# An attention and mixture-of-experts layer on one core: the orders of the repeated step and of the last chunk rewritten on four engines

## What is computed

```python
x = L0_attn_x
xn = _layernorm(x, axis=-1)
# attention
x_tran = jnp.matmul(x, W) + b
weights = jnp.einsum('bsd,btd->bst', x_tran, x)
weights = jnp.exp(jnp.tanh(weights * lw)) * off_diag
weights = weights / (jnp.sum(weights, axis=-1, keepdims=True) + EPS)
return jnp.matmul(weights, x)
# experts: 8, of which the best 2 by sigmoid(x @ gate_w.T) + expert_bias; 176 hidden units each
h = jnp.square(jax.nn.relu(h.astype(jnp.bfloat16)))
routed_out = _masked_grouped_mm(h.astype(jnp.bfloat16), w_down.astype(jnp.bfloat16), onehot)
# shared expert, also 176 hidden units
hs = jnp.square(jax.nn.relu(xf @ shared_w_up.T))
shared_out = hs @ shared_w_down.T
# all of it
x = x + _L0_attn_ref(xn, ...) + _L0_ffn_ref(xn, ...)
```

## Time and profile before

| what | us |
|---|---|
| median of 3 runs (lowest, highest) | 120.36 (120.07, 120.89) |
| the profiled execution | 120.12 |
| its span, first to last instruction | 118.4 |

### The profile page before, as it was taken

How to read it: one execution, slowest core, us unless ns; L and a number is a source line. 1 busy time by engine, 2 the same in 40 slices (tenths; PEclk the granted TensorE clock), 3 DMA queues, 4 the chain that set the end, 5 groups by cost and what they waited for, 6 DMA issues and landing times.

```text
span 118.4 us, 2789 instructions
## 1 busy us (share of the span) xinstructions
PE 110.9 (94%) x912; PEld 84.1 (71%) x912; DVE 99.9 (84%) x316; ACT 89.0 (75%) x138; POOL 71.5 (60%) x121
## 2 busy tenths in 40 slices
PE   3977699999999999999999999999999999999981
PEld 3934346968768786878678776869587876778780
DVE  6996889888898989989888988988988688989821
ACT  4463699798579894989689876989499867996740
POOL 6459798999993389716991499436971603215000
PEclk9999999999999999999999999999999999999999
DMA  3999306628956939296848959393938757696962
GB/s 85 302 239 312 118 0 122 122 41 169 172 111 123 176 73 208 42 214 93 154 89 200 101 108 173 78 179 81 170 77 210 130 110 134 120 213 127 158 174 89
DMA packets 47821, 16.56 MB, mean 140 GB/s; under 512 B 44992, under 2 KB 45760, under 8 KB 47808
## 3 DMA queue, kind: packets, MB, share of 16 engines
q1 hardware_dynamic: 47232, 15.44, 64.8%
q0 software_dynamic: 288, 0.72, 3.5%
q10 hardware_dynamic: 288, 0.23, 0.9%
HBM read 3.84 MB, written 2.10 MB: 50 GB/s over the span
## 4 chain that ended last, share of the span: by engine, by line
PE 86%; DVE 8%; issue 2%; ACT 1%; POOL 1%; DVEq 0%; POOLq 0%; ACTq 0%
PE out_ps L925 16%; PE h_ps L878 14%; PE side L854 11%; PE dots L833 10%; PE out_ps L913 6%; DVE gated L639 5%; PE side L867 5%; PE out_ps L907 4%; PE small L823 4%; PE out_ps L955 4%; PE small L805 4%; PE small L790 2%; PE h_ps L891 2%; PE small L814 1%; PE side L823 1%
## 5 line engine op out<-in xcount | busy, mean ns | idle before, releaser
L639 DVE SCALAR_TENSOR_TENSOR gated<-h_ps,gates 128x1408 bf16<-128x1408 f32 x28 | 45.1, 1612 | 5.0 <-PE h_ps L878 4.5
L467 ACT ACTIVATE hidden<-gated 128x1408 bf16<-128x1408 bf16 x30 | 41.3, 1376 | 2.4 <-DVE gated L654 1.2
L925 PEld LDWEIGHTS out_ps<-downT,hiddenT 128*128 128x128 bf16 x341 | 21.5, 98 | 5.7 <-issue 3.4
L925 PE MATMUL out_ps<-downT,hiddenT 128*128 128x128 bf16 x341 | 23.9, 219 | 0.0
L257 POOL TENSOR_SCALAR xn<-x_sb,meanvar,rstd 128x128 f32<-128x128 f32 x28 | 22.1, 800 | 0.8
L878 PE MATMUL h_ps<-upT,xnTb 128*128 128x512 bf16 (+1 forms) x84 | 21.3, 362 | 0.7 <-DVE gated L639 0.5
L290 POOL TENSOR_SCALAR_AFFINE_SELECT probs<-probs 128x256 f32<-128x256 f32 x16 | 6.6, 411 | 20.0 <-ACT probs L424 20.0
L833 PE MATMUL dots<-projT,xnT 128*128 128x256 f32 x60 | 15.6, 382 | 0.6 <-ACT projT L415 0.6
L854 PEld LDWEIGHTS side<-xn,probs 128*128 128x128 f32 x120 | 15.0, 191 | 1.3 <-issue 0.5
L854 PE MATMUL side<-xn,probs 128*128 128x129 f32 x120 | 15.9, 275 | 0.0
L833 PEld LDWEIGHTS dots<-projT,xnT 128*128 128x128 f32 x60 | 10.7, 190 | 4.5 <-ACT projT L415 2.3
(11 more groups left out here) (105 smaller groups left out, 171.7 us busy)
## 6 DMA issues: line engine op xcount, KB each, us to landing
x_sb<-in_x SPq DMA_DIRECT2D x7, 256.0 KB, 8.8
out_y<-final SPq DMA_DIRECT2D x7, 256.0 KB, 4.1
hiddenT<-hidden SPq DMA_TRANSPOSE x31, 3.7
upT<-in_up POOLq DMA_DIRECT2D x1, 352.0 KB, 7.2
downT<-in_down POOLq DMA_DIRECT2D x1, 352.0 KB, 8.1
out_y<-final SPq DMA_DIRECT2D x2, 128.0 KB, 1.7
late_sb<-in_late SPq DMA_DIRECT2D x1, 192.0 KB, 5.6
x_sb<-in_x ACTq DMA_DIRECT2D x1, 128.0 KB, 2.8
```

Source lines behind the costliest of these rows:

```text
L467: a.activation(hidden[:, t, :], gated[:, t, :], ACT.Square).then_inc(squared, 1)
L639: v.scalar_tensor_tensor(out=gated[:, t, :].rearrange("p (e h) -> p e h", e=E), in0=h_ps[:, 0:NH].rearrange("p (e h) -> p e h", e=E), scal ...
L925: last = t_.matmul(out_at(t), hiddenT[:, c % 2, t, j, :], downT[:, j, :], start=(t == 0 and j == 0 and c < LAST), stop=((t >= 2 or c == LA ...
```

## The change

Nothing is computed differently. The routing scores of chunk 0 are kept in PSUM (`scores_at`), for which the first `route_scores` waits for `decay_copied` and the first `shared_main` for the first gates. POOL's early `normalize` calls are split by tile. Step k = 2 is written out with the calls and the order it had. For k from 3 on, and after the loop for the last chunk, the calls are the same and stand in another order on PE, DVE, ACT and POOL. SP's list stays.

```diff
--- before.py
+++ after.py
@@ -176,6 +176,11 @@
         def out_at(t):
             return out_bank(t // 2)[:, (t % 2) * P:(t % 2 + 1) * P]
 
+        def scores_at(c):
+            if c > 0:
+                return scores[:, :, :]
+            return out_ps[:, 0:TILES * E].rearrange("p (t e) -> p t e", t=TILES)
+
         def turn_at(part):
             return h_ps[:, part * CH:(part + 1) * CH].bitcast(BF16)
 
@@ -329,14 +334,19 @@
             normalize_fourth()
             narrow(0)
             rsqrt(1)
-            normalize(1)
+            normalize(1, 0, 1)
+            normalize(1, 1, 2)
+            normalize(1, 2, 3)
+            normalize(1, 3, 4)
             mask(0, 0)
             narrow(1)
             square_rest(0)
             rsqrt(2)
-            normalize(2, 0, 2)
+            normalize(2, 0, 1)
+            normalize(2, 1, 2)
             mask(0, 1)
-            normalize(2, 2, 4)
+            normalize(2, 2, 3)
+            normalize(2, 3, 4)
             make_gates(1)
             square_rest(1)
             square_shared(0)
@@ -347,21 +357,33 @@
             mask(1, 1)
             narrow_ident()
             narrow(2)
-            for k in range(2, NCH + 1):
...
+            for k in range(3, NCH + 1):
                 f, c = k, k - 1
                 if k + 1 < NCH:
                     rsqrt(k + 1)
+                if f < NCH:
+                    square_rest(f)
+                if k + 1 < NCH:
                     normalize(k + 1)
                 if f < NCH:
-                    square_rest(f)
-                add_x(c)
+                    make_gates(f)
                 square_shared(c)
                 if f < NCH:
-                    make_gates(f)
                     mask(f, 0)
-                    mask(f, 1)
+                add_x(c)
                 if k + 1 < NCH:
                     narrow(k + 1)
+                if f < NCH:
+                    mask(f, 1)
 
         @block.scalar
         def _(act):
@@ -410,6 +432,8 @@
                 a.activation(pair[:, :, 0:2], top8[:, :, 0:2], ACT.Copy).then_inc(pair_set, 1)
 
             def take_proj(c):
+                if c == 0:
+                    act.wait_ge(early_loaded, 16)
                 act.wait_ge(proj_made, c + 1)
                 wait(act, dots_made, Q * (c - 1))
                 a.activation(projT[:, c % 2, :], proj_bank(c)[:, :], ACT.Identity, bias=b_sb).then_inc(proj_taken, 1)
@@ -470,7 +494,6 @@
             take_xT(0)
             copy_decay()
             exp_logits(0)
-            act.wait_ge(early_loaded, 16)
             take_proj(0)
             take_pair(0)
             relu_rest(0)
@@ -496,16 +519,28 @@
             take_exp(1, 1)
             exp_logits(2)
             relu_rest(2)
-            for k in range(2, NCH):
...
+            for k in range(3, NCH):
                 f, c = k, k - 1
+                relu_rest(f)
+                exp_logits(f)
                 scale_attention(c)
-                if f >= 3:
-                    exp_logits(f)
-                    relu_rest(f)
                 square(c, 0)
                 square(c, 1)
+                take_proj(f)
                 take_pair(f)
-                take_proj(f)
                 relu_shared(c)
                 square(c, 2)
                 take_tanh(f, 0)
@@ -515,9 +550,9 @@
                 square(c, 3)
                 take_tanh(f, 1)
                 take_exp(f, 1)
+            scale_attention(LAST)
+            square(LAST, 0)
             relu_shared(LAST)
-            square(LAST, 0)
-            scale_attention(LAST)
             square(LAST, 1)
             square(LAST, 2)
             square_last()
@@ -588,7 +623,9 @@
             def route_scores(c):
                 dve.wait_ge(expT_taken, c + 1)
                 wait(dve, gates_ready, c)
-                v.reciprocal(scores[:, :, :], onep[:, :, :]).then_inc(topk_step, 1)
+                if c == 0:
+                    dve.wait_ge(decay_copied, 1)
+                v.reciprocal(scores_at(c), onep[:, :, :]).then_inc(topk_step, 1)
 
             def route_bias(c):
                 if c == 0:
@@ -597,7 +634,7 @@
                 bias = ebias.rearrange("p (a e) -> p a e", a=1).to_broadcast([P, TILES, E])
                 if c == 0:
                     dve.wait_ge(fillers_set, 2)
-                v.tensor_tensor(biased[:, :, 0:E], scores[:, :, :], bias, ALU.add).then_inc(topk_step, 1)
+                v.tensor_tensor(biased[:, :, 0:E], scores_at(c), bias, ALU.add).then_inc(topk_step, 1)
 
             def route_top(c):
                 then(c, 2)
@@ -615,7 +652,7 @@
 
             def route_gates_first():
                 dve.wait_ge(marks_set, 1)
-                v.scalar_tensor_tensor(out=gates[:, 0, :, :], in0=marked[:, :, 0:E], scalar=MARK, in1=scores[:, :, :],
+                v.scalar_tensor_tensor(out=gates[:, 0, :, :], in0=marked[:, :, 0:E], scalar=MARK, in1=scores_at(0),
                                        op0=ALU.is_equal, op1=ALU.mult).then_inc(gates_ready, 1)
 
             def weigh(c, q):
@@ -725,44 +762,63 @@
             attend_norm(0, 1)
             gate(0, 3)
             weigh(1, 1)
-            for k in range(2, NCH):
...
+            for k in range(3, NCH):
                 f, c, o, g = k, k - 1, k - 2, k + 1
                 gate(c, 0)
                 attend_sums(c, 0)
-                attend_norm(c, 0)
                 if g < NCH:
                     norm_stats(g)
+                attend_norm(c, 0)
                 gate(c, 1)
+                route_one(f)
                 finish(o, 0)
-                route_one(f)
+                route_scores(f)
                 attend_sums(c, 1)
-                route_scores(f)
+                route_bias(f)
                 attend_norm(c, 1)
-                route_bias(f)
                 attend(c)
                 route_top(f)
                 gate(c, 2)
+                weigh(f, 0)
                 route_mark(f)
-                weigh(f, 0)
                 gate(c, 3)
+                weigh(f, 1)
                 finish(o, 1)
-                weigh(f, 1)
             gate_halves(0)
             attend_sums(LAST, 0)
             attend_norm(LAST, 0)
             gate_halves(1)
+            gate_halves(2)
             finish(LAST - 1, 0)
-            gate_halves(2)
             attend_sums(LAST, 1)
+            finish(LAST - 1, 1)
             attend_norm(LAST, 1)
-            finish(LAST - 1, 1)
             gate_halves(3)
-            attend(LAST)
             at, to = PARTS[1]
             dve.wait_ge(turned, 2)
             dve.wait_ge(out_made, TILES * (LAST - 1))
             v.tensor_copy(hiddenT[:, LAST % 2, TILES - 1, at:to, :].rearrange("p j n -> p (j n)"),
                           turn_at(1)[:, 0:(to - at) * P]).then_inc(turned_taken[1], 1)
+            attend(LAST)
             finish(LAST, 0)
             finish(LAST, 1)
 
@@ -859,7 +915,7 @@
             def shared_main(c):
                 if c == 0:
                     pe.wait_ge(late_loaded, 16)
-                    pe.wait_ge(decay_copied, 1)
+                    pe.wait_ge(gates_ready, 1)
                 if c == LAST:
                     pe.wait_ge(proj_taken, c + 1)
                 elif c > 0:
@@ -977,47 +1033,65 @@
             dots(1, 1)
             transpose_x(2)
             down_tile(0, 0)
-            for k in range(2, NCH):
...
+            for k in range(3, NCH):
                 f, c, o = k, k - 1, k - 2
                 up_tile(c, 0)
                 attend(c, 0)
-                if k == 2:
-                    down_tile(0, 1)
+                shared_down_rest(o)
                 rest(f)
-                shared_down_rest(o)
                 up_tile(c, 1)
                 shared_down_main(o)
                 down_tile(o, 2)
                 transpose_exp(f)
                 attend(c, 1)
+                project(f)
                 up_tile(c, 2)
-                project(f)
-                down_tile(o, 3)
                 shared_main(c)
                 dots(f, 0)
+                down_tile(o, 3)
                 up_tile(c, 3)
-                down_tile(c, 0)
                 if f + 1 < NCH:
                     transpose_x(f + 1)
                 dots(f, 1)
+                down_tile(c, 0)
                 down_tile(c, 1)
             c, o = LAST, LAST - 1
             up_by_bank(0)
+            attend(c, 0)
             shared_main(c)
-            attend(c, 0)
             up_by_bank(1)
             shared_down_rest(o)
+            attend(c, 1)
+            up_by_bank(2)
             shared_down_main(o)
-            up_by_bank(2)
             down_tile(o, 2)
-            attend(c, 1)
             down_tile(o, 3)
             up_by_bank(3)
             shared_down_rest(c)
             shared_down_main(c)
             down_tile(c, 0)
+            turn_last()
             down_tile(c, 1)
-            turn_last()
             down_last()
             down_tile(c, 2)
 
```

(76 more changed lines are left out.)

## The result

| | before | after |
|---|---|---|
| median of 17 runs (lowest, highest), us | 120.46 (120.07, 120.98) | 119.69 (119.09, 120.09) |
| the profiled execution, us | 120.12 | 119.69 |
| its span, us | 118.4 | 117.9 |

The ratio of the changed kernel to the one before is 0.9927, with a 95% interval of 0.9909 to 0.9944. That is 0.73% less, or 0.88 us of 120.46 by the ratio; the two medians differ by 0.77. The forecast was 0.88 less and a median of 119.5, so the total is right to within 0.2. The way there is not: one term that was set to zero brought some 0.3 to 0.4, and one that was set to 0.46 was lost, wholly in the profiled execution and in part in others. The profile of the changed kernel shows both.

A forecast was written before the change was run, and what follows sets the result against it. PE was taken as the bound in the middle of the kernel. Steps 0.35 and last chunk 0.53, with the beginning at 0, made 0.88 off 120.36 us: 119.48, rounded 119.5, range 118.9 to 120.5.

The forecast's parts named there:

- PE bounds the steps and only neighbours count: Steps k = 3 to 7: PE's calls stay the same, so only their neighbours matter; 0.35 us less in sum.
- The swap of `rest` and `shared_down_rest` at 0, between -0.1 and +0.2: Steps 3 to 7: exchanging these two calls was priced at 0, with bounds of -0.1 to +0.2 us a step.
- The two close places: Repeated steps: `shared_main` waiting for bank `side`, 0.09 us left, and POOL's `mask` ahead of `attend(f, 0)`, 0.5 left.
- rival E: Steps: POOL's new wait for the marks makes PE's `attend(f, 0)` late; 121.7 us if 0.8 later than counted; chance 0.12.
- B: Gain eaten by a late last transposing DMA, or `shared_main` waiting for its bank in the steps; 120.0 to 120.4; chance 0.19.
- C: Steps: no load was exposed by its neighbour as read, so the order changes nothing there; 119.83 us; chance 0.06.
- The last chunk up to `turn_last`, 0.07: Last chunk: new neighbours for `attend(c, 1)` and `shared_down_main(o)` give net -0.06, rounded up to 0.07 us won.
- The beginning at 0: Beginning: scores in PSUM, split `normalize` and moved waits cost some hundredths either way; taken as 0.
- Rival D: Beginning: keeping the scores in PSUM ends the 0.52 us ahead of the first gate; 119.0 us; chance 0.13.
- The end at 0.46: End: `turn_last` before `down_tile(c, 1)` wins PE's idle 0.46 us, if ACT's square and the last DMA are in time.
- last chunk 0.53 forecast: Whole last chunk: 0.07 up to `turn_last` plus 0.46 at the end, 0.53 us less.
- the prediction's own signs of being wrong: PE idle ahead of `shared_main`, `attend` or the last down tile; swapped calls longer; the 0.52 ahead of the first gate gone.

The follow-up runs named there:

- e3_steps: The kernel before with the new order of steps 3 to 7 alone, beginning and last chunk as before; ratio to before 0.9975.
- e5_swap_back: The changed kernel with `rest(f)` again ahead of `shared_down_rest(o)` in steps 3 to 7; 119.52 us, ratio to before 0.9916.
- e1_scores: The kernel before with the scores of chunk 0 in PSUM and nothing else of the change; ratio to before 0.9961.
- e8_wait: The kernel before with only DVE's added wait for `decay_copied` in chunk 0's `route_scores`, scores left in SBUF; ratio to before 0.9971.
- e9_count63: The changed kernel with the memset of `pair` moved from DVE to POOL, one DVE instruction less ahead of the first gate; median 119.83 us, ratio to before 0.9935.
- e4_last: The kernel before with the new order of the last chunk alone; ratio to before 0.9971.

## Why the prediction came out right, and where it did not

- **PE bounds the steps and only neighbours count: right.** 0.35 forecast, 78.31 - 77.95 = 0.35 measured (78.307 - 77.952) in the changed kernel, and again in e3_steps. It divides as forecast too: 0.06 in each of the steps 3 to 6 and 0.11 in step 7. `shared_main` went from 0.91 to 0.86, `dots` of step 7 from 0.92 to 0.86.
- **The swap of `rest` and `shared_down_rest` at 0, between -0.1 and +0.2: right.** Same middle in e5_swap_back.
- **The two close places: in time.** The residual that frees the bank ended at 69.73 + 0.61 = 70.34, and `shared_main` started at 70.59, with no idle time ahead of it (DVE's timeline, after):

```profile
69.73 0.61 DVE L710 SCALAR_TENSOR_TENSOR resid<-side,rownorm,x_sb 128x128 f32<-128x128 f32 x2
```

  and POOL's timeline, after, shows the new wait for the marks, 1.85 long, and `mask` done at 75.86, where `attend(f, 0)` starts at 76.64, 0.78 later. I had counted 0.5 (my own numbers, 77.14 - 76.5, give 0.64):

```profile
73.86 0.31 POOL L273 TENSOR_SCALAR hot<-marked 128x32 f32<-128x32 f32 x1 [1.85 <-DVE marked L650]
...
75.45 0.41 POOL L295 TENSOR_SCALAR_AFFINE_SELECT probs<-probs 128x256 f32<-128x256 f32 x1
```

  So neither the bank nor the mask was late: rival E did not happen, nor the second half of B. The 0.35 of the steps excludes C.
- **The last chunk up to `turn_last`, 0.07: right, measured 0.06.** `shared_down_rest(c)` starts 8.16 after `up_by_bank(0)`, before 8.22. `attend(c, 1)` pays the 1.09 behind `shared_down_rest` and `shared_down_main(o)` is back at 0.89.
- **The beginning at 0: wrong, the term that was put too low.** Rival D had the place and the size (0.5; measured 0.41 ahead of the gate, 0.33 of it left at `up_tile(1, 0)`, 0.39% in e1_scores), but not the cause. It gave the place of the scores as the reason, and e8_wait and e9_count63 exclude it. The step that failed is "the price is some hundredths either way": the added wait was priced by what it waits for, and not as an instruction that shifts all behind it.
- **The end at 0.46: the move is right, the condition was missed.** The prediction made the gain depend on the landing of the last DMA and put it at the middle, 3.7. It did land in 3.61. But it was issued 0.8 late, because the issue ahead of it on SP took 2.85. I had taken the time of the issue from the square before it and had not asked what holds SP's queue. Rival B had the size: from the end of the square, 109.99, to the landing, 114.41, it is 4.42, and B's 0.6 for a landing of 4.4 is close to the 0.66 measured. Its sentence "the last transpose of the kernel before was in time" is true, but it was read off a kernel in which the packet came too late to hold that issue. How much is lost varies: 0.66 in the profiled execution (tail 16.35), less in those of e5_swap_back, e4_last and e9_count63 (15.99, 15.91, 15.87).
- **The sum.** In the terms of the forecast: steps 0.35 for 0.35; last chunk 0.53 forecast, -0.18 to 0.30 measured; beginning 0 forecast, 0.3 to 0.4 measured. The ratio gives 0.88 in all, the medians 0.77. Two errors of about the same size and opposite sign stand in the right total, and that is luck. Two of the prediction's own signs of being wrong are there: PE idle ahead of the last down tile behind the DMA, and the 0.52 ahead of the first gate gone.

The Trainium skill, "SBUF — State Buffer", section "Who interferes with whom", states that a DVE instruction with two SBUF inputs contends with a GpSimd instruction that reads SBUF. By that rule, keeping the scores in PSUM should free the first gates' making from POOL's `normalize`. No run here shows it. In the kernel before (DVE's timeline):

```profile
12.62 0.19 DVE L618 SCALAR_TENSOR_TENSOR gates<-marked,scores 128x32 f32<-128x32 f32 x1
```

and (POOL's timeline)

```profile
9.69 3.15 POOL L257 TENSOR_SCALAR xn<-x_sb,meanvar,rstd 128x128 f32<-128x128 f32 x4
```

it ran inside POOL's four tiles, which last to 12.84, and took 0.19, and with the scores in PSUM it takes 0.19 as well.

## What to carry to other kernels

Where one engine is busy without a gap, an order can still gain by giving each product whose weights load slowly a neighbour that is long enough to cover the load; such gains are small, but here they could be read from the chain of waits in advance, 0.35 for 0.35. Before work is moved into the last idle stretch of a kernel, look at what that stretch also covers: a DMA that had 0.7 to spare is then on the path, and the queue that issues it has to be read, not only its time to land. An added wait or a moved instruction shifts everything behind it in the list, and in a kernel of 120 us that alone was worth 0.3 to 0.4; an edit that gains should be compared with one that adds only its wait.

## What the runs showed of the hardware

- DVE stood idle for 0.51 to 0.52 ahead of the first gate when 63 recorded instructions lay ahead of it, and for 0.10 to 0.11 with 64, whatever they were.
- Instruction packets of 16 KB, seven in each execution, took 0.88 to 1.85 us. They moved when PE's list was made longer, so I take them for PE's. While the last one was moved in the changed kernel, twenty packets of 256 bytes of a transposing DMA took up to 1.88 us and not 0.02, and the DMA moved next to nothing for 1.5 us. In the ten profiles in which it met that transpose, the transpose landed after 4.5 to 5.2 us, and in the three in which it came earlier, after 3.5 to 3.6. That the two share one of the 16 DMA engines fits this, but no record here names the engine.
- The next issue on SP took 2.39 to 2.85 us in the five profiles in which that packet started 5.76 to 6.45 after `up_by_bank(0)`, and 1.39 to 1.43 in the eight others.
- 48 instructions more on PE (24 products, each with its load) moved the last of these packets from 5.76 after `up_by_bank(0)` to 4.29, and in the kernel before from 7.08 to 4.15; 16 more did not move it.
